# Capacity experts: first expert's rows by a selection product, last expert's rows added by products, output stored tile by tile in the same stage

## The chip, the cores and the metric

The kernel runs on one core of a Trainium2 chip. A core has a matrix engine (TensorE), a vector engine (VectorE), a scalar engine (ScalarE), a general engine (GpSimd) and a queue engine (SyncE) that issues transfers; each has its own instruction stream, and the streams meet only at semaphores. Sixteen transfer engines (DMA) move data between DRAM and the on-chip memory SBUF. TensorE writes into eight accumulator banks (PSUM) of 128 x 512 numbers each. The metric is the time of one execution on the device, in microseconds. All numbers are f32.

## The reference, cut to what matters

Two layers of a perceiver with 8 x 64 = 512 tokens of width 512. The change lies in the very last part, a mixture of 8 experts with a fixed capacity:

```
xf = layernorm(x).reshape(512, 512)
probs = softmax(xf @ Wr);  topk_probs, topk_experts = top_k(probs, 2)
cap = ceil(512 * 2 * 1.25 / 8)              # 160
y = zeros
for e in range(8):
    gate = sum(where(topk_experts == e, topk_probs, 0), -1)
    vals, idx = top_k(where(chosen by e, gate, -inf), cap)
    g = where(isfinite(vals), vals, 0)
    y = y.at[idx].add(g[:, None] * (relu(xf[idx] @ W1[e]) @ W2[e]))   # W1 512x2048, W2 2048x512
out = x + y
```

Each token goes to two experts at most; an expert takes the 160 tokens with the highest gates.

## The kernel before, in words

The program is a row of stages, each with its own tiles and semaphores. At the end of a stage all engines meet, its semaphores are cleared, and they meet again. `capacity_experts` (line 1839) is the last stage that computes; `write_out` (L3033) is a stage of its own that stores `x`, 1 MB, with one transfer and waits for it (L3041).

Tokens lie in 4 tiles (`NT`) of 128 partitions. The stage begins with the norm of `x` into `hn`; SyncE stores `hn` into the DRAM tensor `dispatched` (L1934). TensorE turns `hn`, computes the router's logits (L2149), VectorE makes the gates (`gate`), TensorE spreads each expert's gates over all partitions (L2157), and ScalarE copies them out as `gate_rows`.

For an expert e, `place_tokens(e)` on VectorE (L2010 to L2020) counts for each token how many tokens come before it, and makes `pick`: for each of the four token tiles a matrix of 128 tokens by 160 slots, 1 where the token has that slot. `list_tokens(e)` on TensorE (L2168) multiplies `pick` with gates and token numbers into the bank `meta`; `take_tokens(e)` on VectorE (L2031, L2032) copies each slot's gate and token number. With the numbers GpSimd gathers the expert's rows out of `dispatched`, 128 rows and 32 rows (L1964). `turn_rows(e)` on TensorE (L2181) turns them into the banks `turned`, and `put_picked(e)` on VectorE (L2039) copies them into `picked_T`.

The order on TensorE for each expert is written out by hand at the end of the function: `wide` 0 to 5 (L2198), 64 products of 160 columns against W1 in groups of 12, the last one of 4; between them `turn_y(e - 1)`, and after the third group `list_tokens(e + 1)`; after the sixth `turn_rows(e + 1)`; then `down` 0 and 1 (L2213), 48 and 16 such products against W2. (The calls are the same for each expert; before expert 0 stand `list_tokens(0)` and `turn_rows(0)`.) ScalarE copies each group out of its bank (L2100, L2110), and in `put_y(e)` scales the turned output rows with the slot's gate (L2120) and stores them into the DRAM tensor `expert_rows` (L2124). VectorE's order is also written by hand: `place_tokens(0)`, `take_tokens(0)`, `place_tokens(1)`, `put_picked(0)`, and then per expert the next ones' steps. `find_slots` computes for each token the rows in `expert_rows` of its two experts: the greater and the lesser number, 0 (a row of zeros) where there is none.

At the end GpSimd gathers, per token tile, first the lesser slot's rows (k = 1) and then the greater's (k = 0) (L1976), and VectorE adds them to `x` (L2076). The gathers of k = 1 wait until experts 0 to 6 are stored, those of k = 0 until all are.

SyncE loads the weights in chunks of 2 MB, three places for each of W1 and W2 (L1920, L1926); a chunk's place is free when the products that read it are done.

Of the kernel before, what the change touches and what calls it, by code (L numbers as in the profile page):

```python
# [1838 lines left out]
def capacity_experts(g):  # L1839
# [12 lines left out]

    W1_READ, W2_READ = (3, len(TRIPLES)), (len(TRIPLES) + 1, N_RING)
    with Stage(nc, "f") as s:
        w1 = s.sb("w1", [P, CHUNKS, KD, F // 2])
# [31 lines left out]
        slot = s.sb("slot", [P, TOP, NT], mybir.dt.uint32)  # L1887
        back = s.sb("back", [P, NT, D])
        ring = [s.ps(f"ring{i}", [P, 512]) for i in range(3)]
        meta = s.ps("meta", [P, 512])  # L1890
        turned = [s.ps(f"turned{i}", [P, 512]) for i in range(2)]
        y_back = [s.ps(f"y_back{i}", [P, D]) for i in range(2)]
        acc = turned + y_back
        r_in = s.sem("r_in")
        w1_in = [s.sem(f"w1_in{i}") for i in range(CHUNKS)]
# [14 lines left out]
        gathered = [s.sem(f"gathered{t}") for t in range(NT)]  # L1910
        added = s.sem("added")
        block = s.block()

        @block.sync
        def _(sp):
# [24 lines left out]
            for e in range(E_N):  # L1940
                for n in (2 * e + 3, 2 * e + 4):
                    if n < 2 * E_N:
                        load_w1(n)
                for n in (2 * e + 3, 2 * e + 4):
                    if n < 2 * E_N:
                        load_w2(n)

        @block.gpsimd
        def _(pool):
# [6 lines left out]
            pool.wait_ge(hn_stored, 16)  # L1956
            for e in range(E_N):
                pool.wait_ge(tokens_ready, e + 1)
                if e >= 2:

                    pool.wait_ge(picked_full, e - 1)
                for j, (lo, hi) in enumerate(PARTS):
                    m = hi - lo
                    pool.indirect_dma_start(out=rows_in[0:m, e % 2, j, :], out_offset=None, in_=g.dispatch_dram[:, :],  # L1964
                                            in_offset=bass.IndirectOffsetOnAxis(ap=token[0:m, e % 2, j:j + 1], axis=0)
                                            ).then_inc(rows_landed[e % 2], 16)
            pool.wait_ge(slots_ready, 1)
            pool.wait_ge(zero_stored, 16)
            for k in (1, 0):

                pool.wait_ge(y_stored[0], 32 * E_N // 2)
                pool.wait_ge(y_stored[1], 32 * (E_N // 2 - k))
                for t in range(NT):
# [7 lines left out]
        def _(dve):  # L1981
# [41 lines left out]
            def take_tokens(e):  # L2023
                dve.wait_ge(tokens_full, e + 1)
                if e >= 2:

                    dve.wait_ge(rows_landed[e % 2], 32 * (e // 2))
                    dve.wait_ge(y_out, 2 * (e - 1))
# [7 lines left out]
            def put_picked(e):  # L2036
                dve.wait_ge(picked_full, e + 1)
                for j, (lo, hi) in enumerate(PARTS):
                    dve.tensor_copy(picked_T[:, e % 2, :, lo:hi],  # L2039
# [3 lines left out]
            def find_slots():  # L2043
# [8 lines left out]
                own.wait()  # L2052
                own.did(dve.tensor_reduce(slot_f[:, 0, :], kept[:], AXX, ALU.max))
                own.did(dve.tensor_reduce(slot_f[:, 1, :], kept[:], AXX, ALU.add))
                own.wait()
# [3 lines left out]

            place_tokens(0)  # L2060
            take_tokens(0)
            place_tokens(1)
            put_picked(0)
            for e in range(E_N):
# [8 lines left out]
            for k in (1, 0):  # L2073
                for t in range(NT):
                    dve.wait_ge(gathered[t], 16 * (2 - k))
                    dve.tensor_tensor(g.x[:, t, :], back[:, t, :], g.x[:, t, :], ALU.add).then_inc(added, 1)  # L2076

        @block.scalar
        def _(act):
# [33 lines left out]
            def put_y(e):  # L2113
                act.wait_ge(tokens_ready, e + 1)
                for j, (lo, hi) in enumerate(PARTS):
                    m = hi - lo
                    act.wait_ge(y_full, 2 * e + j + 1)
                    if e >= 2:
                        act.wait_ge(y_stored[e % 2], 32 * (e // 2))
                    act.activation(y[0:m, e % 2, j, :], y_back[j][0:m, :], ACT.Copy, scale=slot_gate[0:m, e % 2, j:j + 1]  # L2120
                                   ).then_inc(y_out, 1)
                act.wait_ge(y_out, 2 * e + 2)
                for j, (lo, hi) in enumerate(PARTS):
# [3 lines left out]
            for e in range(E_N):  # L2127
# [4 lines left out]
                for n in range(2, len(TRIPLES)):  # L2132
                    put_hidden(e, n)
                for j in range(len(DOWN)):
                    put_y_T(e, j)
            put_y(E_N - 1)

        @block.tensor
        def _(pe):
# [21 lines left out]
            def list_tokens(e):  # L2161
# [8 lines left out]
                last.then_inc(tokens_full, 1)  # L2170

            def turn_rows(e):
                pe.wait_ge(rows_landed[e % 2], 32 * (e // 2 + 1))
                if e >= 1:
                    pe.wait_ge(picked_out, 2 * e)
                else:
                    pe.wait_ge(rows_out, E_N)
                for j, (lo, hi) in enumerate(PARTS):
# [39 lines left out]
            def turn_y(e):  # L2218
# [3 lines left out]
                for j, (lo, hi) in enumerate(PARTS):  # L2222
                    for k in range(KD):
                        last = pe.transpose(y_back[j][0:hi - lo, k * P:(k + 1) * P], y_T[:, k, lo:hi], g.ident[:])  # L2224
                    last.then_inc(y_full, 1)

            pe.wait_ge(numbered, 1)
            list_tokens(0)
            turn_rows(0)
            for e in range(E_N):  # L2230
# [11 lines left out]
                for j in range(len(DOWN)):  # L2242
                    down(e, j)
            turn_y(E_N - 1)

# [786 lines left out]

def write_out(g):  # L3033
    nc = g.nc
    with Stage(nc, "z") as s:
        stored = s.sem("stored")
        block = s.block()

        @block.sync
        def _(sp):  # L3040
            sp.dma_start(tokens(g.out), g.x[:]).then_inc(stored, 16)  # L3041
            sp.wait_ge(stored, 16)


def constants(g):
# [18 lines left out]
def build(nc, dram, out, stages=range(6)):  # L3064
    with ExitStack() as ctx:
# [23 lines left out]
        if 5 in stages:  # L3089
            capacity_experts(g)  # L3090
        write_out(g)

# [94 lines left out]
```

## Time and profile before

| | us |
|---|---|
| median of three runs | 2594.85 (2593.65 to 2602.11) |
| profiled execution, its time | 2598.24 |
| profiled execution, span from the first to the last instruction | 2596.5 |
| the stage of the capacity experts and the output store | about 2222 to 2596.5 |

The busy shares, the chain of waits and the timelines are of that profiled execution. Its time is 1.7 us longer than its span. An f32 product of the code stands in the trace as two instructions of TensorE, a transpose as one. "Idle before" in a timeline row is the time that the engine stood still ahead of the row, and the arrow names what ended it.

### The profile page before, as it was taken

Reading aid. Unit: us, or ns where it says so; the run is one execution under the profiler, and the core shown is the slowest. Engines: PE = TensorE matmul, PEld = TensorE weight load, DVE = VectorE, ACT = ScalarE, POOL = GpSimd, SP = SyncE. Lnnn points to the kernel's source line nnn. Section 1 sums busy time; section 2 is a strip of 40 time slices with the busy share of each in tenths; the row PEclk is TensorE's granted clock in tenths of the full one; section 3 lists DMA queues with packets and bytes.
Section 4 is the critical chain, followed back from the end, with each engine's and each line's share of the span. In section 5 each row is a group of like instructions: output and inputs, shape, how many; then the busy total and the mean of one; then the engine's idle time right before and its main releaser. Section 6 shows DMA issues by size and latency. Waiting matters only on the chain. (4 is left out here: it accounts for less than half of the span.)

```text
span 2596.5 us, 26998 instructions
## 1 busy us (share of the span) xinstructions
PE 2236.0 (86%) x10194; PEld 1341.1 (52%) x10194; DVE 1044.8 (40%) x2135; ACT 735.0 (28%) x1462; POOL 421.4 (16%) x477
## 2 busy tenths in 40 slices
PE   5799999999999885799999878776898966599996
PEld 2355555555555433444444435444454434499996
DVE  4345655655655025200000258777294035422110
ACT  2334544544444112211111143342153101111111
POOL 0000000000000000489993111222000000000001
PEclk8999999999999997799999988776899987799998
DMA  5001222122121220868877364231400010556552
GB/s 193 26 15 47 72 74 64 52 75 75 41 70 54 93 73 21 315 261 315 314 309 282 131 212 134 95 114 39 171 33 16 0 66 2 218 210 242 218 207 92
DMA packets 131539, 327.33 MB, mean 126 GB/s; under 512 B 39857, under 2 KB 89170, under 8 KB 111827
## 3 DMA queue, kind: packets, MB, share of 16 engines
q1 hardware_dynamic: 99392, 297.20, 31.7%
q10 hardware_dynamic: 29202, 19.49, 2.4%
q0 software_dynamic: 2816, 8.92, 1.0%
q8 instruction: 83, 1.36, 0.2%
q14 instruction: 46, 0.37, 0.0%
HBM read 303.22 MB, written 21.24 MB: 125 GB/s over the span
## 5 line engine op out<-in xcount | busy, mean ns | idle before, releaser
L868 PE MATMUL a_mix<-a_xn,a_probs_T 128*128 128x384 f32 (+1 forms) x832 | 313.4, 493 | 14.3 <-issue 10.2
L797 PE MATMUL a_sc<-a_wk_centred,a_ctx_T 128*128 128x512 f32 x624 | 288.3, 599 | 4.3 <-DVE a_keys L462 2.3
L1774 PE MATMUL c_gate_up<-c_w_wide,c_h_rows 128*128 128x512 f32 x480 | 210.9, 592 | 0.0
L868 PEld LDWEIGHTS a_mix<-a_xn,a_probs_T 128*128 128x128 f32 (+1 forms) x832 | 145.5, 191 | 119.8 <-issue 72.3
L797 PEld LDWEIGHTS a_sc<-a_wk_centred,a_ctx_T 128*128 128x128 f32 x624 | 117.9, 192 | 129.2 <-issue 106.0
L1679 DVE TENSOR_TENSOR c_hidden<-c_silu,c_gate_up 128x512 f32<-128x512 f32 x38 | 26.1, 688 | 355.1 <-PE c_gate_up L1774 343.3
L2198 PE MATMUL f_ring<-f_picked_T,f_w 128*128 128x160 f32 x1024 | 146.6, 304 | 1.0 <-DVE f_picked_T L2039 1.0
L1774 PEld LDWEIGHTS c_gate_up<-c_w_wide,c_h_rows 128*128 128x128 f32 x480 | 90.1, 190 | 108.1 <-issue 108.1
L462 DVE SCALAR_TENSOR_TENSOR a_keys<-a_k_bias,a_std,a_sc 128x512 f32<-128x512 f32 (+1 forms) x104 | 77.1, 742 | 167.6 <-PE a_sc L797 167.6
L2198 PEld LDWEIGHTS f_ring<-f_picked_T,f_w 128*128 128x128 f32 x1024 | 142.9, 193 | 1.3 <-DVE f_picked_T L2039 1.1
L2213 PE MATMUL f_ring<-f_hidden,f_w 128*128 128x160 f32 x1024 | 141.2, 300 | 0.4 <-ACT f_hidden L2100 0.4
L2213 PEld LDWEIGHTS f_ring<-f_hidden,f_w 128*128 128x128 f32 x1024 | 139.3, 190 | 0.9 <-ACT f_hidden L2100 0.6
L1817 PE MATMUL c_y<-c_w_down,c_hidden_T 128*128 128x512 f32 x304 | 138.9, 601 | 0.0
L616 ACT ACTIVATE a_sq<-a_keys 128x512 f32<-128x512 f32 (+1 forms) x104 | 65.6, 630 | 195.3 <-DVE a_keys L462 195.3
L421 POOL TENSOR_SCALAR a_mask<-a_mask 128x896 bf16<-128x896 uint8 x8 | 7.5, 937 | 614.6 <-DVE a_top L491 596.5
L2707 PE MATMUL d_mean<-d_share,d_scores 128*128 128x64 f32 (+1 forms) x416 | 75.3, 372 | 33.3 <-issue 24.3
L491 DVE CUSTOM_DVE_ANT_0 a_probs<-a_sc,a_mask 128x896 f32<-128x896 f32 x64 | 67.3, 1088 | 82.1 <-PE a_sc L828 82.1
L2707 PEld LDWEIGHTS d_mean<-d_share,d_scores 128*128 128x128 f32 (+1 forms) x416 | 74.0, 284 | 34.5 <-issue 24.5
L2542 POOL TENSOR_TENSOR d_scores<-d_scores,d_left 128x1601 f32<-128x1601 f32 x16 | 54.0, 3374 | 213.1 <-ACTq L2616 212.8
L2560 DVE MAX8 d_best<-d_left 128x8 f32<-128x1601 f32 x48 | 87.6, 1826 | 1.4
L2564 DVE MATCH_REPLACE8 d_left<-d_best,d_left 128x1601 f32<-128x1601 f32 x48 | 86.9, 1811 | 0.0
L1817 PEld LDWEIGHTS c_y<-c_w_down,c_hidden_T 128*128 128x128 f32 x304 | 55.9, 194 | 56.4 <-issue 56.4
(489 smaller groups left out, 3505.6 us busy)
## 6 DMA issues: line engine op xcount, KB each, us to landing
c_w_wide<-in_L_ffn_W SPq DMA_DIRECT2D x68, 1024.0 KB, 7.0
f_w<-in_L_ffn_W SPq DMA_DIRECT2D x32, 2048.0 KB, 9.5
c_w_down<-in_L_ffn_W SPq DMA_DIRECT2D x34, 1024.0 KB, 7.5
a_ctx_T<-in_ctx_T SPq DMA_DIRECT2D x48, 384.0 KB, 3.6
a_xn<-in_ctx SPq DMA_DIRECT2D x24, 768.0 KB, 6.4
d_context_T<-in_ctx_T SPq DMA_DIRECT2D x24, 768.0 KB, 10.5
d_context<-in_ctx SPq DMA_DIRECT2D x8, 2304.0 KB
mixed_context<-a_mixed_T ACTq DMA_DIRECT2D x84, 64.0 KB, 1.8
```

Of the source, the lines that this page charges most:

```text
L462: dve.scalar_tensor_tensor(out=keys[0:m, n % 4, :], in0=k_bias[0:m, :], scalar=std[0:m, t:t + 1], in1=key_bank(b, t)[0:m, :], op0=ALU.mult ...
L491: dve.tensor_tensor_reduce(out=probs[:, n % 2 * 2 + h, :].rearrange("p (c n) -> p c n", c=2), in0=sc[h][:, :, 0:BANK], in1=mask[:].rearran ...
L616: act.activation(sq[0:m, n % 2, :], keys[0:m, n % 4, :], ACT.Square).then_inc(squared, 1)
L797: last = pe.matmul(key_bank(b, t), ctx_T[:, n % AHEAD, k, cols], wk_centred[:, k, :], start=(k == 0), stop=(k == KC - 1))
L868: ins = pe.matmul(mix[:, 0:DC], probs_T[0:m, t, p * P:(p + 1) * P], xn[0:m, b % 2, t, :], start=(t == 0), stop=(t == CT - 1))
L1774: last = pe.matmul(gate_up[2 * (u % 2) + part][:], h[:, k, :], w_wide[:, i % WIDE_RING, k, :], start=(k == 0), stop=(k == KD - 1))
L1817: last = pe.matmul(y[t % 2][:], hidden_T[:, u % 2, k, :], w_down[:, i % DOWN_RING, k, :], start=(c == 0 and k == 0), stop=(c == 1 and k == ...
L2198: last = pe.matmul(ring[use % 3][:, (m - lo) * CAP:(m - lo + 1) * CAP], w1[:, i % CHUNKS, k, at:at + P], picked_T[:, e % 2, k, :], start=( ...
L2213: last = pe.matmul(ring[use % 3][:, (m - lo) * CAP:(m - lo + 1) * CAP], w2[:, i % CHUNKS, k, at:at + P], hidden[:, k, :], start=(k == 0), ...
L2560: own.did(dve.max(eight, src))
L2564: ins = dve.match_replace(left[:, r, :], eight, src, MASKED)
L2707: last = pe.matmul(mean[t // 8][0:m, t % 8, :], scores[:, b % KEEP, r, t * P:t * P + m], share[:, r, :], start=(r == 0), stop=(r == 1))
```

## The change

Three things are changed, all at the two ends of the last stage.

The first expert's rows are no longer gathered. TensorE multiplies `hn` (as weights, 128 tokens by 128 features) with `pick` of expert 0 (160 columns), 4 x 4 products, which gives the rows already turned in the banks `turned`. GpSimd's gathers begin with expert 1; the buffers and waits are counted accordingly.

The last expert's rows are no longer stored and gathered. Its `pick` is turned by eight transposes between the two `down` steps, ScalarE copies it out as `pick_T`, and at the end eight products of 512 columns (4 token tiles, slots in two parts of 128 and 32) put the scaled rows into four banks, which VectorE adds to `x`. `find_slots` leaves out the last expert, so the k = 1 gathers need the rows of experts 0 to 5, and the k = 0 gathers those of 0 to 6.

The output is stored by SyncE in four transfers, one per tile after its last addition, inside the stage; the stage `write_out` is gone.

```diff
+    LAST = E_N - 1
+    def landed(e):
+        return 32 * (e // 2 + e % 2)
+        pick_T = s.sb("pick_T", [P, 2, TOK])
+        put = [turned[0], turned[1], meta, ring[0]]
 # SyncE, behind the weight loads
+            for t in range(NT):
+                sp.wait_ge(summed, t + 1)
+                sp.dma_start(tokens(g.out)[:, t, :], g.x[:, t, :]).then_inc(stored, 16)
+            sp.wait_ge(stored, 16 * NT)
 # GpSimd
-            for e in range(E_N):
+            for e in range(1, E_N):
                 pool.wait_ge(tokens_ready, e + 1)
-                if e >= 2:
+                if e >= 3:
                     pool.wait_ge(picked_full, e - 1)
...
             for k in (1, 0):
-                pool.wait_ge(y_stored[0], 32 * E_N // 2)
-                pool.wait_ge(y_stored[1], 32 * (E_N // 2 - k))
+                pool.wait_ge(y_stored[0], 32 * (E_N // 2 - k))
+                pool.wait_ge(y_stored[1], 32 * (E_N // 2 - 1))
 # VectorE
-                    dve.wait_ge(rows_landed[e % 2], 32 * (e // 2))
+                    if e >= 3:
+                        dve.wait_ge(rows_landed[e % 2], landed(e - 2))
...
             def put_picked(e):
                 dve.wait_ge(picked_full, e + 1)
+                if e == 0:
+                    for j, (lo, hi) in enumerate(((0, 3), (3, KD))):
+                        dve.tensor_copy(picked_T[:, 0, lo:hi, :], turned[j][:, 0:(hi - lo) * CAP]
+                                        .rearrange("p (k n) -> p k n", k=hi - lo)).then_inc(picked_out, 1)
+                    return
...
-                own.did(dve.tensor_reduce(slot_f[:, 0, :], kept[:], AXX, ALU.max))
+                own.did(dve.tensor_reduce(slot_f[:, 0, :], kept[:, :, 0:LAST], AXX, ALU.max))
...
             place_tokens(0)
+            put_picked(0)
             take_tokens(0)
             place_tokens(1)
-            put_picked(0)
...
+            dve.wait_ge(added, 2 * NT)
+            for t in range(NT):
+                dve.wait_ge(put_full, t + 1)
+                dve.tensor_tensor(g.x[:, t, :], put[t][:], g.x[:, t, :], ALU.add).then_inc(summed, 1)
 # ScalarE: put_y(LAST) returns after the scaling; no store
-                for j in range(len(DOWN)):
-                    put_y_T(e, j)
+                put_y_T(e, 0)
+                if e == LAST:
+                    act.wait_ge(pick_turned, 1)
+                    for j, (lo, hi) in enumerate(PARTS):
+                        act.activation(pick_T[0:hi - lo, j, :], turned[j][0:hi - lo, :], ACT.Copy).then_inc(pick_T_out, 1)
+                put_y_T(e, 1)
 # TensorE
+            def pick_rows():
+                pe.wait_ge(rows_out, E_N)
+                pe.wait_ge(picks_ready, NT)
+                for k in range(KD):
+                    j, at = divmod(k * CAP, 3 * CAP)
+                    for t in range(NT):
+                        last = pe.matmul(turned[j][:, at:at + CAP], g.hn[:, t, k * P:(k + 1) * P], pick[:, 0, t, :],
+                                         start=(t == 0), stop=(t == NT - 1))
+                last.then_inc(picked_full, 1)
...
+            def turn_pick():
+                pe.wait_ge(picked_out, 2 * E_N)
+                for j, (lo, hi) in enumerate(PARTS):
+                    for t in range(NT):
+                        last = pe.transpose(turned[j][0:hi - lo, t * P:(t + 1) * P], pick[:, LAST % 2, t, lo:hi],
+                                            g.ident[:])
+                last.then_inc(pick_turned, 1)
+
+            def put_rows():
+                pe.wait_ge(pick_T_out, 2)
+                pe.wait_ge(tokens_ready, E_N)
+                for j, (lo, hi) in enumerate(PARTS):
+                    pe.wait_ge(y_out, 2 * LAST + j + 1)
+                    for t in range(NT):
+                        last = pe.matmul(put[t][:], pick_T[0:hi - lo, j, t * P:(t + 1) * P], y[0:hi - lo, LAST % 2, j, :],
+                                         start=(j == 0), stop=(j == 1))
+                        if j == 1:
+                            last.then_inc(put_full, 1)
+
             pe.wait_ge(numbered, 1)
+            pick_rows()
             list_tokens(0)
-            turn_rows(0)
...
                 for j in range(len(DOWN)):
                     down(e, j)
-            turn_y(E_N - 1)
+                    if e == LAST and j == 0:
+                        turn_pick()
+            turn_y(LAST)
+            put_rows()
 # build
-        write_out(g)
```

## Rows read from the trace of the kernel before

**Rows 1.** The page, busy time, share of the span and instructions of each engine.

```profile
PE 2236.0 (86%) x10194; PEld 1341.1 (52%) x10194; DVE 1044.8 (40%) x2135; ACT 735.0 (28%) x1462; POOL 421.4 (16%) x477
```

**Rows 2.** The chain of waits in order of time: start, duration in us, what.

```profile
2243.64 0.77 DVE f_compared L2010 x2
...
2250.17 0.95 DVE f_pick L2020 x4
```

**Rows 3.** Timeline of TensorE, capacity stage: start, duration in us, instructions [idle before].

```profile
2241.86 1.97 PE L2157 MATMUL f_turned<-ident,f_gate 128*128 128x128 f32 x8 [4.20 <-DVEq L2000]
...
2251.26 1.55 PE L2168 MATMUL f_meta<-f_gate,f_pick 128*128 128x2 f32 x16 [4.02 <-DVE f_pick L2020]
2263.76 1.68 PE L2181 MATMUL f_turned<-ident,f_rows_in 128*128 128x128 f32 x8 [10.95 <-DMA f_rows_in<-dispatched,f_token]
2266.42 13.07 PE L2198 MATMUL f_ring<-f_picked_T,f_w 128*128 128x160 f32 x72 [0.98 <-DVE f_picked_T L2039]
...
2288.76 1.02 PE L2181 MATMUL f_turned<-ident,f_rows_in 128*128 128x128 f32 x8 [0.33 <-DMA f_rows_in<-dispatched,f_token]
2289.71 17.65 PE L2213 MATMUL f_ring<-f_hidden,f_w 128*128 128x160 f32 x128
...
2405.86 1.02 PE L2181 MATMUL f_turned<-ident,f_rows_in 128*128 128x128 f32 x8 [2.06 <-DMA f_rows_in<-dispatched,f_token]
...
2521.42 1.02 PE L2181 MATMUL f_turned<-ident,f_rows_in 128*128 128x128 f32 x8 [1.43 <-DMA f_rows_in<-dispatched,f_token]
```

**Rows 4.** Windows: stretch, length, engines' busy time; last three: granted clock, DMA share, GB/s.

```profile
2245.00:2246.00 1.00, 1.00 (x10) 1.00 (x9) 0.94 (x4) 0.79 (x2) 0.00 (x0) 0.84 1.00 426
2251.00:2252.00 1.00, 0.74 (x7) 0.77 (x7) 0.12 (x1) 0.00 (x0) 0.00 (x0) 1.00 1.00 426
2252.00:2253.00 1.00, 0.81 (x11) 0.71 (x10) 0.15 (x3) 0.00 (x0) 0.00 (x0) 0.57 0.96 410
...
2266.40:2272.65 6.25, 6.23 (x23) 6.23 (x24) 0.00 (x0) 0.00 (x0) 0.00 (x0) 0.50 0.00 0
...
2273.00:2274.00 1.00, 1.00 (x9) 1.00 (x9) 0.00 (x0) 0.57 (x1) 0.00 (x0) 1.00 0.00 0
...
2579.00:2580.00 1.00, 0.00 (x0) 0.00 (x0) 0.00 (x0) 0.00 (x0) 0.00 (x0) 0.91 0.41 158
```

**Rows 5.** The weights' tile, its loads issued between 2224 and 2232.

```profile
DMA to landing us min/median/max: 10.3/20.6/32.6
```

**Rows 6.** Groups by line and shape (count, busy us, mean ns), and one timeline row of VectorE.

```profile
L1347 PE MATMUL e_ring<-e_wo,e_o_T 128*128 128x512 f32 x32 | 14.0, 595 | 0.7 <-ACT e_o_T L1266 0.7
...
L2039 DVE COPY f_picked_T<-f_turned 128x512 f32<-128x512 f32 x8 | 5.5, 690 | 21.0 <-PE f_turned L2181 21.0
...
L2039 DVE COPY f_picked_T<-f_turned 128x128 f32<-128x128 f32 x8 | 2.2, 280 | 0.0
...
2221.04 0.69 DVE L1235 TENSOR_TENSOR x<-e_ring,x 128x512 f32<-128x512 f32 x1 [2.74 <-PE e_ring L1347]
```

**Rows 7.** The chain of waits at the end, in order of time.

```profile
2576.72 0.67 PE f_y_back L2224 x4
...
2578.05 0.67 ACT f_y L2120
...
2579.10 1.90 DMA expert_rows<-f_y
...
2585.79 3.71 DMA f_back<-expert_rows,f_slot
...
2589.53 0.69 DVE x L2076
```

**Rows 8.** SyncE's timeline, and transfers by line: size in KB, median us from issue to landing.

```profile
2591.46 0.40 SPq L3041 DMA_DIRECT2D out<-x  x1
...
expert_rows<-f_y ACTq DMA_DIRECT2D x8, 256.0 KB, 2.1
...
out<-x SPq DMA_DIRECT2D x1, 1024.0 KB, 4.3
```

More of the change, by code:

```diff
@@ L1910, in capacity_experts @@
         gathered = [s.sem(f"gathered{t}") for t in range(NT)]
-        added = s.sem("added")
+        added, pick_turned, pick_T_out = s.sem("added"), s.sem("pick_turned"), s.sem("pick_T_out")
+        put_full, summed, stored = s.sem("put_full"), s.sem("summed"), s.sem("stored")
         block = s.block()
@@ L2052, in find_slots @@
                 own.wait()
-                own.did(dve.tensor_reduce(slot_f[:, 0, :], kept[:], AXX, ALU.max))
-                own.did(dve.tensor_reduce(slot_f[:, 1, :], kept[:], AXX, ALU.add))
+                own.did(dve.tensor_reduce(slot_f[:, 0, :], kept[:, :, 0:LAST], AXX, ALU.max))
+                own.did(dve.tensor_reduce(slot_f[:, 1, :], kept[:, :, 0:LAST], AXX, ALU.add))
                 own.wait()
@@ L2121, in put_y @@
                                    ).then_inc(y_out, 1)
+                if e == LAST:
+                    return
                 act.wait_ge(y_out, 2 * e + 2)
@@ L2133, in _ @@
                     put_hidden(e, n)
-                for j in range(len(DOWN)):
-                    put_y_T(e, j)
-            put_y(E_N - 1)
+                put_y_T(e, 0)
+                if e == LAST:
+                    act.wait_ge(pick_turned, 1)
+                    for j, (lo, hi) in enumerate(PARTS):
+                        act.activation(pick_T[0:hi - lo, j, :], turned[j][0:hi - lo, :], ACT.Copy).then_inc(pick_T_out, 1)
+                put_y_T(e, 1)
+            put_y(LAST)
         @block.tensor
@@ L2170, in list_tokens @@
                 last.then_inc(tokens_full, 1)
-            def turn_rows(e):
[L2173 to L2177, printed above, removed]
+            def pick_rows():
[7 more added lines that the diff above has]
+                last.then_inc(picked_full, 1)
+            def turn_rows(e):
+                pe.wait_ge(rows_landed[e % 2], landed(e))
+                pe.wait_ge(picked_out, 2 * e)
                 for j, (lo, hi) in enumerate(PARTS):
@@ L3030, in _ @@
             ss.on_gpsimd(pool)
[L3033 to L3042, printed above, removed]
 def constants(g):
```

## The prediction

> **What bounds the kernel now.** I read the busy shares first: TensorE is busy for 86% of the span, VectorE for 40%, ScalarE for 28% [rows 1]. The reader is to see that no other engine can be the bound on average, and that this says nothing yet of the two ends of the last stage, which is where the change works.
>
> Then the chain of waits, in order of time, and TensorE's timeline beside it. Before the first expert the chain goes through VectorE (eight comparisons, then four picks, ready at 2251.13), a small product on TensorE that lists the tokens, and GpSimd's two gathers [rows 2, 3]. The list is done at 2252.8, the turning of the gathered rows starts at 2263.76 after 10.95 us of idle time, and the first weight product at 2266.42. From there to about 2577.8 TensorE runs almost without a break: seven more gathers leave four gaps, 0.33 us the first, 2.06 the longest, 1.43 the last, 4.2 us in all [rows 3]. The end of the chain is again not TensorE: turning the last expert's output back (2576.72), scaling on ScalarE (to 2578.72), store to DRAM (1.90), four gathers, the last one landing 3.71 us after its issue, and the last addition, 2589.53 to 2590.22 [rows 7]. The output store is issued at 2591.46 and takes 4.3 us, and the span ends at 2596.5, 0.74 us later [rows 8].
>
> The granted clock is the third view. After TensorE began to turn the gates at 2241.86 it rose at about 2245.2; it is 1.00 when the list starts and falls to half (1.2 GHz) within the next microsecond, after TensorE had idled for 4.0 us. After the long wait it is 0.50 until 2272.65: the first 23 instructions took 6.23 us, 0.27 us each. At 2.4 GHz 128 of them take 17.65 us, 0.138 each [rows 3, 4]. One thing has to be seen in the counts: 36 products of the first three groups stand there as 72 instructions [rows 3]. An f32 product is two passes; a transpose is one.
>
> **The head: the first expert's rows by a product.** Removed from the path: two gathers, eight turnings. Added: 16 products of 160 columns, so 32 instructions, from 2251.26 on, where the list started before. Bounds: 32 at 0.138 are 4.4 us, 32 at 0.27 are 8.7. Until the clock falls, at about 2252.15, six run at 0.138; at half clock some 13 more run until 2255.6, where I let it rise, since TensorE works without a break here and the turning of the gates got the clock back in 3.4 us [rows 3, 4]; the last 13 take 1.8 us: done at 2257.3. The list follows (1.3 to 1.56 us): 2258.7. VectorE's two copies out of the banks (480 and 160 elements, about 0.95 us by the copies of 512 and 128 at 0.69 and 0.28 [rows 6]) run beside the list and end at 2258.3, hidden by 0.4 us; were the cover gone, they would cost 0.95. First weight product at 2258.7 instead of 2266.42: **7.7 us gained**.
>
> The clock gives the rest. The first 72 instructions took 13.07 us, where 72 at 0.138 are 9.9 [rows 3]. If the clock is up before they start, **3.2 us** more are gained; if it stays low as long behind their start as before, nothing, and then the selection is the slow one too. So the head gives 10.9; its bounds are 5.8 (the 8.7 us selection and a low clock behind it) and 12.6 (no fall at all: 1.7 us less than I count for the selection).
>
> What is late next? The weights: the six chunks issued from 2224 to 2232 land 10.3 to 32.6 us after their issue, the last by about 2264 [rows 5]. The first expert's second chunk is wanted 64 instructions after the start, at 2267: cost 0. The picks of the second expert: VectorE now waits for the selection before it takes the tokens, and behind that waiting copy are queued the first token list and the placing of expert 1, 7.5 us (2243.64 to 2251.13 for the same work [rows 2]). Tokens taken at 2259.1, placed at 2266.6; TensorE wants them after 72 instructions, at 2268.6: hidden by 2.0 us, and by more at a lower clock. Seven gathers stay, each beside 56 instructions as before, 7.7 us; I take their 4.2 us of gaps as unchanged.
>
> **The gathers into the output.** The lesser slot's four gathers need no row of expert 6 any more and go out right behind those of the last expert's rows, in the same GpSimd queue, one expert earlier. Nothing on TensorE's path waits for them, and all eight additions from gathers end before the last product. Cost 0; if they delay the rows in front, the price of rival 2. The reductions over seven experts in place of eight: 0.
>
> **The tail: the last expert's rows by products.** Between the two halves of the last down-projection TensorE gets eight transposes, 1.02 us in the row of eight [rows 3]; I take 0.9, on the path. ScalarE's two copies of them (0.67 us each, as its scaling [rows 7]) lie beside the 32 instructions that follow, 4.4 us: 0. The turning back starts at 2577.6, and the first scaled part is out at 2579.05 (the second scaling started at 2578.05 before [rows 7], plus 0.9 and a little). Then come eight products of 512 columns, 16 instructions at 14.0/32 = 0.44 us [rows 6]: 7.0 us, with 0.15 for the drain of the last (0.595 long, 0.44 apart), to 2586.2. The second part's scaling ends beside the first four. VectorE adds a tile out of its bank in 0.69 us [rows 6], less than the 0.875 in which TensorE fills the next, so only the last addition follows: 2586.9, where it was 2590.22. The gain is small because 7.15 + 0.7 us of products and addition replace 1.90 + 3.71 us of transfers, the gathers' issues and an addition.
>
> The output goes in four stores of 256 KB; only the last is on the path. Such a store landed in 2.1 us, one of 1 MB in 4.3 [rows 8]. The stage's exit, which stood between the last addition and the store (1.24 us with the entry of the next stage), now comes behind the store, where the exit was 0.74 us; I take 1.0. End: 2586.9 + 2.1 + 1.0 = 2590.0: **6.4 us gained** (6.7 with an exit of 0.74). The products' clock is the open term: in the trace it is still up after the turning and has begun to fall before 2580 [rows 4], when TensorE had stood still for 2 us. It now works there, so I take it as held. If it falls for 3.4 us and comes back as in the head, 1.7 us are lost; if it falls and stays low, 6.1, and the tail gives 0.3.
>
> **Sum.** 7.7 + 3.2 + 6.4 = 17.3 us. The profiled execution took 2598.24 us (span 2596.5 and 1.7 around it): 2580.9. It lies 3.4 us above the median of the three runs with the same work on the path, so the predicted time is 2594.85 - 17.3 = **2577.5 us**. Own range of this case, with the difference between runs of one kernel: 2573 to 2581.
>
> **The rivals.**
> 1. The clock is low at both ends: 5.8 in the head and 0.3 in the tail: 6.1, 2588.8 us, no change that can be measured. For it: the trace fell at just these two places [rows 4]. Against: TensorE then had nothing to do. The Trainium skill speaks for it: "TensorE: Matmul & The Clock Gate", section "A second HAM failure mode: psum-queue depth-cycling", tells of a kernel whose short idle times between groups of products make the clock swing. By that rule the tail's products, which stand behind short waits for ScalarE, would run at half clock at least in part; no row here shows it; both falls in these rows stand behind idle times of 2 us and more.
> 2. The lesser slot's gathers collide with the last expert's rows: 4 x 128 rows more while a weight chunk is also under way. Price: what the first gather paid when the transfer engines were full [rows 4], 10.95 us of idle TensorE in place of 1.43 [rows 3], 9.5 us. Against: they are queued behind. 2587.0 us.
> 3. Only the tail's clock falls and stays low: 10.9 + 0.3 = 11.2: 2583.7 us.
> 4. Slower than before: the seven gathers left come late and the clock falls at each. With the first gather's 10.95 us against the cover of 7.7 each leaves 3.2 us, and a fall behind it costs 3.2 more, as at the first expert: 6.4 for each of seven, 45 less the 4.2 there are, against 17.3 gained: 2618 us. It decides from the fourth of the seven on (4 x 6.4 = 25.6 against 21.5). Against: they have the same products and the same weight loads beside them as before, and their longest gap is 2.06 us.
> 5. More than forecast: no fall in the head and the short exit, 12.6 + 6.7 = 19.3: 2575.6 us.
>
> **How the numbers follow.** Chances: forecast 0.58, rival 1 0.09, rival 2 0.08, rival 3 0.10, rival 4 0.03, rival 5 0.12. No change means within 0.3% (7.8 us), about what a measurement of this kernel can tell: rival 1 with a part of rival 2, which lies on the border, 0.12. Slower: rival 4, 0.03. Faster: 0.85. The range reaches from below rival 5, by a few microseconds in which runs of one kernel differ (2593.65 to 2602.11 before), to rival 2's border: 2571 to 2586.
>
> **What would show it.** Right: no gather before the first weight product, which starts 7.4 us after the first selection instruction and runs at 0.138 from the start; no idle time before the second expert's list; 16 instructions of 512 columns at the end, 0.44 apart; the last store landing 2 us after its issue; 12.8 us from the last weight product to the end of the span instead of 20.2. Wrong: granted clock 0.5 in the first group or in the last products, idle time before the second expert's list (VectorE late), a gap of several microseconds before the last expert's rows are turned, or an exit far over 1 us.

## The result: 13 us faster by the medians, 15.7 us in the stage of the two profiles

| | median, us | range | ratio to before, 95% interval |
|---|---|---|---|
| before, 8 runs | 2594.25 | 2590.33 to 2606.17 | |
| changed, 8 runs | 2580.85 | 2575.23 to 2591.23 | 0.9948 [0.9925, 0.9971] |
| before, beside e1 to e4, 23 runs | 2601.43 | 2592.01 to 2605.20 | |
| changed again (e4 below), 6 runs | 2584.78 | 2578.86 to 2588.73 | 0.9943 [0.9921, 0.9964] |

The ratio is that of the times beside each other on one chip, and not exactly the quotient of the medians. The predicted gain of 17.3 us lies inside the interval (7.5 to 19.5 us). The predicted time was 2577.5; the median is 3.4 us above it. The runs of one kernel differ by 16 us, and most of that seems to arise before the stage that was changed: in the thirteen profiles of this study it starts anywhere from 2218.4 to 2233.5 us, though the code ahead of it is the same, while the stage took 358.2 and 355.4 us in the two profiles of the changed kernel. So times are compared here from the stage's first instruction (the norm's statistics on VectorE) to the end of the span. The page of the changed kernel, busy shares as in [rows 1]:

```profile
span 2579.9 us, 27075 instructions
PE 2248.7 (87%) x10242; PEld 1349.2 (52%) x10242; DVE 1047.1 (41%) x2139; ACT 736.6 (29%) x1464; POOL 419.8 (16%) x475
```

TensorE is busy 12.7 us longer than before (1.7 of that in a slow row, see below) and the kernel is faster: most of its added work stands where the core waited. Its timeline answers to [rows 3] (start, duration, instructions, idle time ahead):

```profile
2250.35 6.26 PE L2207 MATMUL f_turned<-f_pick,hn 128*128 128x160 f32 x32 [3.82 <-DVE f_pick L2033]
2256.44 1.29 PE L2197 MATMUL f_meta<-f_gate,f_pick 128*128 128x2 f32 x16
2257.66 10.05 PE L2234 MATMUL f_ring<-f_picked_T,f_w 128*128 128x160 f32 x72
2267.55 1.29 PE L2197 MATMUL f_meta<-f_gate,f_pick 128*128 128x2 f32 x16
...
2277.01 1.02 PE L2217 MATMUL f_turned<-ident,f_rows_in 128*128 128x128 f32 x8 [0.36 <-DMA f_rows_in<-dispatched,f_token]
...
2509.26 1.02 PE L2217 MATMUL f_turned<-ident,f_rows_in 128*128 128x128 f32 x8 [1.50 <-DMA f_rows_in<-dispatched,f_token]
2510.20 19.33 PE L2249 MATMUL f_ring<-f_hidden,f_w 128*128 128x160 f32 x128
...
2561.33 1.04 PE L2267 MATMUL f_turned<-ident,f_pick 128*128 128x128 f32 x8
2562.20 4.51 PE L2249 MATMUL f_ring<-f_hidden,f_w 128*128 128x160 f32 x32
2567.11 1.09 PE L2260 MATMUL f_y_back<-ident,f_y_T 128*128 128x128 f32 x8 [0.39 <-ACT f_y_T L2133]
2568.69 1.96 PE L2277 MATMUL f_turned<-f_y,f_pick_T 128*128 128x512 f32 x4 [0.48 <-ACT f_y L2143]
...
2572.29 1.98 PE L2277 MATMUL f_turned<-f_y,f_pick_T 32*128 32x512 f32 x4
...
2574.97 1.02 PE L2277 MATMUL f_ring<-f_y,f_pick_T 32*128 32x512 f32 x2
```

Three things are to be seen. The first weight product comes 7.31 us after the first selection instruction, with no idle time between, where 15.16 us lay before; 72 instructions then take 10.05 us, not 13.07. The second expert's list follows with no idle time ahead of it, so VectorE was in time. And one row is worse than any of before: the 128 down instructions of expert 6 take 19.33 us instead of 17.65; such a group is called slow in what follows.

The end, VectorE's last additions and the output's stores (transfers: size in KB, median us to landing), beside [rows 7, 8]:

```profile
2573.52 1.48 DVE L2099 TENSOR_TENSOR x<-f_turned,x 128x512 f32<-128x512 f32 x2 [24.01 <-PE f_turned L2277]
2575.16 0.69 DVE L2099 TENSOR_TENSOR x<-f_meta,x 128x512 f32<-128x512 f32 x1 [0.17 <-PE f_meta L2277]
2576.02 0.69 DVE L2099 TENSOR_TENSOR x<-f_ring,x 128x512 f32<-128x512 f32 x1 [0.17 <-PE f_ring L2277]
...
out<-x SPq DMA_DIRECT2D x4, 256.0 KB, 2.0
```

Additions wait for TensorE (0.17 us each); the last ends at 2576.71, 10.0 us after the last weight instruction (2566.71) instead of 13.9, and the span ends 3.2 us later instead of 6.3. The two profiles add up:

| part of the span | before | changed | difference |
|---|---|---|---|
| ahead of the stage | 2222.62 | 2221.70 | -0.9 |
| stage's start to first selection or list instruction | 28.64 | 28.65 | 0 |
| to the first weight product | 15.16 | 7.31 | -7.9 |
| first 72 weight instructions | 13.07 | 10.05 | -3.0 |
| from there to the last weight instruction | 296.8 | 299.0 | +2.2 |
| to the last addition | 13.9 | 10.0 | -3.9 |
| to the end of the span | 6.3 | 3.2 | -3.1 |

Of the +2.2 us, 0.9 are the eight transposes and 1.7 the slow row, less 0.4 of shorter gaps.

The -3.0 us of the first 72 instructions hold for this profile of the kernel before. e2 and e3 (below) keep its head as it was, and there the same 72 took less, because the clock came back 3.5 and 2.9 us after their start and not 6.25 us after it [rows 4]. TensorE's timeline of e2, a window of it (the third number from the end is the granted clock), and the timeline of e3:

```profile
2262.08 11.69 PE L2212 MATMUL f_ring<-f_picked_T,f_w 128*128 128x160 f32 x72 [0.98 <-DVE f_picked_T L2043]
```

```profile
2265.00:2266.00 1.00, 1.00 (x7) 1.00 (x6) 0.00 (x0) 0.00 (x0) 0.00 (x0) 0.77 0.00 0
```

```profile
2267.57 11.44 PE L2202 MATMUL f_ring<-f_picked_T,f_w 128*128 128x160 f32 x72 [0.98 <-DVE f_picked_T L2043]
```

From the first list instruction to the end of the 72, the old head took 28.2, 26.7 and 26.4 us in the three profiles that have it, and the new one 17.4 (18.4 in e1): 9.1 to 10.9 us for the head of the changed kernel, by the execution that one compares with.

### The profile page after: what moved, and what is told of

Its sections match the earlier page's. It is cut to its first block and busy times, and to the rows that moved or that the text cites. A ratio compares the mean times of both kernels' runs of the same rounds, so it can differ in the third digit from the quotient of the medians.

```text
span 2579.9 us, 27075 instructions
## 1 busy us (share of the span) xinstructions
PE 2248.7 (87%) x10242; PEld 1349.2 (52%) x10242; DVE 1047.1 (41%) x2139; ACT 736.6 (29%) x1464; POOL 419.8 (16%) x475
## 5 line engine op out<-in xcount | busy, mean ns | idle before, releaser
L868 PE MATMUL a_mix<-a_xn,a_probs_T 128*128 128x384 f32 (+1 forms) x832 | 315.1, 496 | 13.9 <-issue 9.8
```

Of the source, the lines that this page charges most:

```text
L868: ins = pe.matmul(mix[:, 0:DC], probs_T[0:m, t, p * P:(p + 1) * P], xn[0:m, b % 2, t, :], start=(t == 0), stop=(t == CT - 1))
```

## The experiments

Each run is told by its ratio to the kernel before on the same chip and by the stage of its profiled execution. The columns: stage's start to the end of the span; first selection or list instruction to the first weight product; first 72 weight instructions; the gaps ahead of the turned rows of experts 1 to 7, summed; down groups of 128 that took 19.33 us instead of 17.65; last weight instruction to last addition; from there to the end. There is one profile for each kernel. Pauses ahead of the down products are not among the gaps: 1.09 us in e4 and 0.61 in e9 ahead of those of expert 6, 1.49 in e5 ahead of those of the last expert, where the changed kernel has 0.39.

| kernel | ratio [95%] | stage | to weights | 72 | gaps | slow | to add | to end |
|---|---|---|---|---|---|---|---|---|
| before | | 373.9 | 15.16 | 13.07 | 4.21 | 0 | 13.9 | 6.28 |
| changed | 0.9948 [0.9925, 0.9971] | 358.2 | 7.31 | 10.05 | 3.84 | 1 | 10.0 | 3.19 |
| e1 head only | 0.9943 [0.9924, 0.9962] | 361.6 | 8.37 | 10.05 | 2.22 | 0 | 13.6 | 6.28 |
| e2 tail product | 0.9986 [0.9970, 1.0001] | 370.8 | 15.01 | 11.69 | 4.22 | 1 | 10.0 | 6.06 |
| e3 store tiles | 0.9994 [0.9977, 1.0011] | 369.3 | 14.98 | 11.44 | 2.88 | 0 | 15.8 | 3.13 |
| e4 changed again | 0.9943 [0.9921, 0.9964] | 355.4 | 7.32 | 10.05 | 1.42 | 0 | 10.4 | 3.18 |
| e5 gathers late | 0.9948 [0.9929, 0.9966] | 355.1 | 7.32 | 10.05 | 1.21 | 0 | 10.2 | 3.21 |
| e6 kept warm | 0.9947 [0.9925, 0.9968] | 358.3 | 5.65 | 10.05 | 5.16 | 1 | 10.0 | 3.19 |
| e7 list early | 0.9941 [0.9918, 0.9964] | 351.8 | 7.32 | 10.05 | 0 | 0 | 10.2 | 3.18 |
| e8 all three | 0.9932 [0.9910, 0.9955] | 349.7 | 5.65 | 10.05 | 0.28 | 0 | 10.0 | 3.24 |
| e9 one store | 0.9957 [0.9941, 0.9973] | 357.2 | 7.32 | 10.05 | 1.39 | 0 | 10.3 | 5.41 |
| e10 warm twice | 0.9930 [0.9914, 0.9946] | 350.2 | 5.65 | 10.05 | 0.72 | 0 | 10.0 | 3.25 |
| e11 all three again | 0.9924 [0.9908, 0.9939] | 350.1 | 5.64 | 10.05 | 0.67 | 0 | 10.0 | 3.25 |

### e1: the head alone

The kernel before with `pick_rows`, gathers from expert 1 on, and VectorE's new order:

```diff
-            list_tokens(0)
-            turn_rows(0)
+            pick_rows()
+            list_tokens(0)
```

> Kernel before with the selection product alone; last expert and output as before. Theory (the parts add up): the first weight product 7.3 us after the first selection instruction and the first 72 weight instructions in 10 us, so the profile 10.9 us shorter between the picks and the second expert's list, ratio to before about 0.9958. Rival (the tail's change carries the gain, the head's is given back as longer gaps before the turning of the later experts' rows): the gaps of experts 1 to 7 add up to 10 us and more instead of 4, ratio 1.000.

The stage is 12.3 us shorter, 9.8 of it at the place of the change (15.16 + 13.07 against 8.37 + 10.05), and the gain was not given back as gaps: 2.2 us. The rival is refuted. The theory holds but for 1.1 of its 10.9 us: the first weight product comes 8.37 us after the selection's start and not 7.3. The ratio can't tell e1 from the whole change. The selection took 1.06 us longer than in the changed kernel. The windows say why (the third number from the end is the granted clock):

```profile
2256.00:2257.00 1.00, 0.00 (x0) 0.00 (x0) 0.93 (x7) 0.00 (x0) 0.00 (x0) 0.56 1.00 426
2257.00:2258.00 1.00, 0.61 (x2) 0.64 (x3) 0.25 (x2) 0.00 (x0) 0.00 (x0) 0.50 1.15 492
...
2262.00:2263.00 1.00, 1.00 (x5) 1.00 (x5) 0.00 (x0) 0.00 (x0) 0.00 (x0) 0.52 1.07 459
2263.00:2264.00 1.00, 1.00 (x10) 1.00 (x9) 0.00 (x0) 0.00 (x0) 0.00 (x0) 1.00 1.15 492
```

Here the clock had fallen before the selection began and came back at 2263.0, 5.6 us after; in the changed kernel it fell during it:

```profile
2250.00:2251.00 1.00, 0.65 (x5) 0.68 (x6) 0.20 (x1) 0.00 (x0) 0.00 (x0) 1.00 0.88 377
2251.00:2252.00 1.00, 1.00 (x8) 1.00 (x8) 0.00 (x0) 0.00 (x0) 0.00 (x0) 0.82 1.11 475
2252.00:2253.00 1.00, 1.00 (x6) 1.00 (x5) 0.00 (x0) 0.00 (x0) 0.00 (x0) 0.50 1.04 442
...
2255.00:2256.00 1.00, 1.00 (x9) 1.00 (x8) 0.00 (x0) 0.00 (x0) 0.00 (x0) 0.97 1.04 442
```

### e2: the last expert's product alone

The kernel before with `turn_pick`, `put_rows` and the reductions over seven experts; the output stored by `write_out`.

> Kernel before with the last expert's rows put back by products alone; gathers for all other experts, output stored in its own stage. Theory: last weight product to last addition 9.9 to 10 us instead of 13.9, 0.9 us given back for the eight transposes, so 3 us net, ratio 0.9988. Rival (eight f32 products are as dear as the round trip through DRAM): distance 13 us or more, ratio 1.000 or above. In both the lesser slot's gathers move ahead; if these alone cause the clock to fall once after the last expert's rows, this run shows a slower stretch of 3.4 us in the down products of expert 6.

13.9 us became 10.0, less 0.87 for the transposes: 3.0 us, as the theory said, in the profile; the interval of the ratio (0.9970 to 1.0001) doesn't exclude that nothing was gained. Products cost less than the way through DRAM, though eight f32 products of 512 columns take 7.3 us. One slow group is there, but not behind the last expert's rows: it stands in expert 3, behind a gap of 1.89 us, long before any gather into the output.

### e3: the store by tile alone

```diff
+            for t in range(NT):
+                sp.wait_ge(added, NT + t + 1)
+                sp.dma_start(tokens(g.out)[:, t, :], g.x[:, t, :]).then_inc(stored, 16)
+            sp.wait_ge(stored, 16 * NT)
```

> Kernel before with only the output stored by tile in the capacity stage, last expert by gathers. Theory: the last addition to the end of the span takes 2.1 us for the last store and 1.0 for the exit, 3.1 us instead of 6.3, so 3.2 us, ratio 0.9988. Rival (the four stores cost as much as one, since each pays its fixed time): 5 to 6 us, ratio 0.9998.

The last addition to the end is 3.1 us, exactly as forecast, and yet the theory fails for the whole: the last addition itself comes 1.9 us later after the last weight instruction (15.8 us). The additions, whose last wait was 0.53 us before the change, now wait longer and longer for the gathers (0.81, 1.05 and 2.12 us):

```profile
2583.33 0.69 DVE L2080 TENSOR_TENSOR x<-f_back,x 128x512 f32<-128x512 f32 x1 [24.70 <-DMA f_back<-expert_rows,f_slot]
2583.77 1.07 POOL L1980 DMA_INDIRECT f_back<-expert_rows,f_slot  x1 [0.30 <-issue]
2584.05 6.39 SPq L1949 DMA_DIRECT2D out<-x  x4
...
2586.57 0.69 DVE L2080 TENSOR_TENSOR x<-f_back,x 128x512 f32<-128x512 f32 x1 [1.05 <-DMA f_back<-expert_rows,f_slot]
2589.38 0.69 DVE L2080 TENSOR_TENSOR x<-f_back,x 128x512 f32<-128x512 f32 x1 [2.12 <-DMA f_back<-expert_rows,f_slot]
```

The last gather lands 5.6 us after its issue, 3.71 in [rows 7]: the first tile's store, issued at 2584.05, runs beside it. From issue to addition the four gathers took 3.3, 3.6, 4.1 and 5.6 us, against 3.4, 3.6, 3.8 and 3.7 before: the first two as before, the third 0.3 us longer and the last, which had the stores beside it nearly all the time, 1.9. In e1, where the store comes last as well, the last gather took 3.72 us. So the stores are the likely cause, though in one profile. Of 3.15 us saved at the end only 1.3 is left (scaling's end to the end of the span, 17.8 and 16.5 us), and the ratio, 0.9994, can't tell it from nothing. Only together with the product, which takes the gathers away from the end, does the store by tile pay in full: 3.0 and 1.3 us alone, 6.1 together. The parts don't add up as I had said.

### e4: the changed kernel again

> The changed kernel unchanged, beside its parts on the same chip. Theory (parts add up): the gain is the sum of the three runs before it, 10.9 + 3.0 + 3.2 = 17 us, ratio 0.9934, less 1.7 us where the clock falls once more in the middle. Rival (something in the middle eats a part in each execution): the gap ahead of the last expert's rows is longer than before and the 128 down products behind it take 19 us instead of 17.65 again, ratio 0.995.

The stage is 18.5 us shorter than before, more than the forecast's 17.3: gaps of 1.4 us, no slow group. The rival (the middle eats a part each time) is refuted; the slow group does not come in every execution. The last addition is 0.4 us later here, because the clock fell before the last products had ended (timeline, then a window):

```profile
2576.57 1.42 PE L2277 MATMUL f_ring<-f_y,f_pick_T 32*128 32x512 f32 x2
```

```profile
2577.00:2578.00 1.00, 0.99 (x2) 0.00 (x0) 0.46 (x1) 0.00 (x0) 0.00 (x0) 0.53 0.92 344
```

### e5: the lesser slot's gathers held

```diff
-                pool.wait_ge(y_stored[0], 32 * (E_N // 2 - k))
+                pool.wait_ge(y_stored[0], 32 * E_N // 2)
```

> The changed kernel with the lesser slot's gathers held until expert 6 is stored, as before the change. Theory (the gathers' time is a matter of luck with the transfer engines, not of what is queued behind them): the wait ahead of the last expert's rows stays in 0 to 2 us as in the changed kernel, whose two profiles had 1.50 and 0.21; no slower and no faster, ratio to the changed kernel 1.000. Rival (the moved gathers collide with the last expert's rows): this wait falls to under 0.3 us, the down products of expert 6 take 17.65, the time falls by 1 to 3 us.

Stage 355.1 us against 355.4 and 358.2. The wait ahead of the last expert's rows is 0.19 us. With the gathers moved ahead it was 1.50, 0.21, 1.25 (e2), 1.13 (e6) and 0 (e9); with them late 1.43, 0, 0.54 and 0.19. That excludes a collision of 9.5 us, as rival 2 had it, and not one of half a microsecond. Between its own theory and rival the run does not decide: a wait under 0.3 us, 17.65 us for the down products behind it and a stage 0.3 to 3.1 us shorter fit both. The slow group stood behind the last expert's rows in two of five profiles with the gathers moved ahead (changed, e6) and in none of four with them late, which is too few to tell.

### e6: TensorE kept busy while it waits for the picks

```diff
+            for i in range(10):
+                pe.matmul(ring[0][:, 0:CAP], g.ident[:], g.hn[:, i % NT, 0:CAP], start=True, stop=True)
             pick_rows()
```

> The changed kernel with ten idle products of 160 columns into an unused bank while TensorE waits for the first picks (their result is not used). Theory (the selection's 6.3 to 7.3 us is 4.4 of work and a fall of the clock, caused by the 4 us of idle time ahead of it): the granted clock stays 1.00 from the turning of the gates into the weight products, the selection takes 4.4 us, the first weight product comes 5.5 us after the first selection instruction instead of 7.3 to 8.4; 1.9 us or more off the time. Rival (the f32 selection is slow by itself, the weights being another tile each time): it still takes 6 us and more at a granted clock of 1.00.

The timeline of TensorE, then the windows:

```profile
2258.10 2.88 PE L2284 MATMUL f_ring<-hn,ident 128*128 128x160 f32 x20
2262.09 4.58 PE L2207 MATMUL f_turned<-f_pick,hn 128*128 128x160 f32 x32 [1.11 <-DVE f_pick L2033]
2266.52 1.29 PE L2197 MATMUL f_meta<-f_gate,f_pick 128*128 128x2 f32 x16
```

```profile
2258.00:2262.00 4.00, 2.99 (x23) 2.74 (x21) 3.77 (x13) 1.06 (x3) 0.00 (x0) 1.00 1.00 426
2262.00:2267.00 5.00, 4.91 (x38) 4.94 (x38) 0.28 (x1) 0.00 (x0) 0.00 (x0) 1.00 1.00 429
```

The clock stays at 2.4 GHz through the selection, which takes 4.6 us where it took 6.26 and 7.31: the first weight product comes 5.65 us after the selection's start, 1.7 us sooner. Of the 6.26 us, 1.7 were the clock and nothing of the products; e8, e10 and e11 show the same 4.58 us. The rival (slow by itself) is refuted. In this execution the middle gave it back (5.2 us of gaps, one slow group), so the stage's length does not show it; e8 and e11 do.

### e7: the token list one group earlier

```diff
                 wide(e, 1)
+                if 1 <= e < LAST:
+                    list_tokens(e + 1)
                 wide(e, 2)
-                if e + 1 < E_N:
+                if e == 0:
                     list_tokens(e + 1)
```

> The changed kernel with the token list of experts 2 to 7 made one group of weight products earlier (3.3 us). Theory (what the middle loses is gathers that come after 56 instructions of cover, and a fall of the clock behind the longer ones): the waits ahead of the turned rows are zero for experts 2 to 7, every 128 down instructions take 17.65 us, 2 to 5 us faster than the changed kernel. Rival (the gathers only land later, because they meet the load of the next chunks): the same waits, no change.

All seven waits are gone, every group takes 17.65 us, and the stage is 351.8 us, 3.6 to 6.4 less than the changed kernel's. The rival falls: the gathers land in time once they are asked for 3.3 us sooner. In the medians the gain over the changed kernel is not to be seen (ratio 0.9941 against 0.9948 and 0.9943).

### e8 and e11: all three

The edits of e6 and e7, and `turn_pick` ahead of the last expert's down products, where TensorE waits 0.4 us for ScalarE.

> The changed kernel with the idle products, the early list, and the last expert's pick turned ahead of its down products, in the pause in which TensorE waits for ScalarE (0.4 us). Theory: 1.9 (clock held) + 3 (waits gone) + 0.4 (pause used) = 5 us faster than the changed kernel, ratio to the kernel before 0.992. Rival (they share one cause and don't add up): no better than the better of the two runs before it.

> The kernel with the three edits once more, more rounds. Theory: stage's start to its end 350 us instead of 355 to 358 in the changed kernel and 374 before; ratio to the kernel before 0.991, the whole of it in this stage. Rival: the rest of the program varies more than these 8 us, and the ratio lies above 0.994.

Stage 349.7 and 350.1 us; ratios 0.9932 and 0.9924, median 2577.08 us in e11's six runs beside 2598.33 of the kernel before. The kernel beats the one before by 24 us in the stage and the changed one by 5 to 8.5 us, and it beats e7 by 1.7 to 2.1: so the rival of e8 falls, the edits do add up. The ratio of e11 lies between what its theory and its rival said. The intervals of the ratios overlap those of the changed kernel (0.9943, 0.9948), so that gain over the change rests on the stage's length, which e7, e8, e10 and e11 show alike. The one gap left (0.28 and 0.67 us) is that of expert 1, whose list could not move.

### e9: one store of 1 MB in the same stage

```diff
-            for t in range(NT):
-                sp.wait_ge(summed, t + 1)
-                sp.dma_start(tokens(g.out)[:, t, :], g.x[:, t, :]).then_inc(stored, 16)
-            sp.wait_ge(stored, 16 * NT)
+            sp.wait_ge(summed, NT)
+            sp.dma_start(tokens(g.out), g.x[:]).then_inc(stored, 16)
+            sp.wait_ge(stored, 16)
```

> The changed kernel with the output stored by one transfer of 1 MB after the last addition, still inside the capacity stage. Theory (the tail's saving on the store is the size of the last transfer, not the stage that is gone): the store takes 4.3 us and the exit 1.1, so 5.3 us from the last addition to the end instead of 3.2 in the changed kernel and 6.1 to 6.3 with a stage of its own. Rival (the stage that is gone saves it): 3.5 us.

5.41 us from the last addition to the end: the theory holds (5.3), the rival (3.5) is refuted. So of the 2.9 us between e2 (6.06) and the changed kernel (3.19), 2.2 are the smaller last transfer and 0.65 the stage that is gone.

### e10: idle products ahead of the gates too

Six more idle products while TensorE waits for the first gates.

> The kernel with the three edits (idle products, early list, pick turned in the pause) and six further idle products while TensorE waits for the first gates (their result is not used). Theory: the clock rises before the gates are turned, the first four of these take 0.9 us less 0.3, and the picks come 0.3 to 0.5 us earlier after the stage's start than the 28.64 us of all runs so far, the rest as in the kernel with the three edits; 0.4 us faster, not to be told by the time. Rival: the products are still running at half clock when the gates are ready and delay them, 28.7 us and more.

The picks come 28.64 us after the stage's start, as in eleven of the other twelve profiles to 0.02 us: nothing gained, and the theory falls. (In e1, without such products, they came after 28.30 us: there the clock stood high for more of the router's products, which took 4.30 us and not 4.71 as in the changed kernel.) TensorE's timeline shows why nothing was gained, the turning of the gates still ran at half clock:

```profile
2246.30 3.55 PE L2182 MATMUL f_ring<-hn,ident 128*128 128x160 f32 x12
2250.65 1.97 PE L2188 MATMUL f_turned<-ident,f_gate 128*128 128x128 f32 x8 [0.80 <-DVEq L2013]
```

The first turning takes 1.97 us as without the idle products [rows 3]; the fill cost nothing and brought nothing. The rival falls too: the twelve added instructions end 0.80 us before the gates are ready.

## Why the prediction came out

The direction and the mechanism hold, and the size of the two ends against the profile on which it was worked out. By its steps:

- Head, forecast 7.7 + 3.2 = 10.9 us; 7.9 + 3.0 in the profiles. The selection was to be 32 instructions, six at the high clock, then a fall and a return after some 3.4 us: the clock fell at about 2251.6, after some nine instructions, and returned at 2255.1, and the selection took 6.1 us to the list against 6.0 forecast. That the fall lay as forecast is in part luck: in e1 it came before the selection, and the selection took 7.31 us, all but the last eleven instructions at half clock. The bound of 4.4 is nearly e6's 4.58. The 3.2 us for the clock behind the start belong to the one execution on record: against e2 and e3 they would be 1.6 and 1.4.
- VectorE late for the second expert: no idle time ahead of the list in any run.
- Tail, forecast 6.4: 3.9 and 3.1 less 0.9 for the transposes are 6.1. The products took 7.3 us, the last store 2.0 us, the exit 1.2. From the last weight product to the end of the span it was 13.2 us against 12.8 forecast. The open term went the forecast's way: the clock held through the products and fell at about 2575.9, as the last one ended. In four of the ten profiles with these products (e4, e5, e7, e9) it fell up to 0.9 us before their end, at a cost of 0.2 to 0.4 us. In the windows of the changed kernel:

```profile
2574.00:2575.00 1.00, 1.00 (x4) 0.40 (x3) 0.90 (x2) 0.00 (x0) 0.00 (x0) 1.00 0.00 0
2575.00:2576.00 1.00, 0.98 (x3) 0.15 (x1) 0.69 (x1) 0.00 (x0) 0.00 (x0) 0.96 0.83 307
2576.00:2577.00 1.00, 0.00 (x0) 0.00 (x0) 0.69 (x1) 0.00 (x0) 0.00 (x0) 0.50 0.87 322
```

- So rival 1 is refuted for the tail, and with it what was drawn from the Trainium skill ("TensorE: Matmul & The Clock Gate", section "A second HAM failure mode: psum-queue depth-cycling"): pauses of 0.39 and 0.48 us between the groups did not keep the clock low here; at most the last products lost it. Rival 1's head is refuted as well: the first 72 instructions took 10.05 us in every profile with the selection.
- Two prices of that rival don't follow from its rows. With 8.7 us for the selection the head would give 5.0 us and not 5.8, and sixteen instructions at twice 0.44 us would cost the tail 7.0 us and not 6.1. Both make rival 1 slower still and change nothing in the forecast.
- The middle, forecast as unchanged, is where the first profile lost: 1.7 us by a fall of the clock behind the longest gap. The step "I take their 4.2 us of gaps as unchanged" was too dear and blind to that fall: with the head changed and the lists at their old place, the gaps were 3.84, 2.22, 1.42, 1.21, 5.16 and 1.39 us, 2.5 on average, where the three profiles with the old head have 4.21, 4.22 and 2.88. Rival 4 named a late gather and then a fall, and that did happen, once in seven experts and not four times. That the gap is the cause of the fall is not shown: three of the nine profiles with gaps in the middle have a slow group, and none of the four in which the lists were moved.
- Rival 2: of its 9.5 us there is no trace (1.50 us at most ahead of the last expert's rows).

The two ends gave 17.0 us where 17.3 were forecast, and the medians still differ by only 13.4. Some 1.5 to 1.8 us of that are the head of the one profile on which the forecast was worked out: against e2's and e3's heads the two ends give 15.5 and 15.2. The rest lies within the spread of the middle and of the stages ahead, about which no experiment was made; that the medians came as close as they did is also a matter of that spread.

## What to carry to other kernels

A selection matrix that is already there can replace a gather at the first and the last step of a pipeline, where nothing covers the gather; in the middle it hides behind other work. Count f32 products as two instructions each, and look for the clock ahead of them, not only for their length. Splitting the final store paid in full here only where no gather was still under way: two changes at one end must be tried together as well as apart.

## What was not expected of the hardware

- Whether the clock falls behind a short gap is not settled by the length of the gap. Behind the waits ahead of the turned rows it fell after 1.13 (e6), 1.50 (changed) and 1.89 us (e2), each time for about 3.4 us and at a cost of 1.7, and held after 1.25 (e2), 1.43 and 2.06 (before) and 1.68 (e3), and after the 1.49 us of e5 ahead of the down products. In the changed kernel it came 1.8 us after the gap had ended, while TensorE was working:

```profile
2510.00:2511.00 1.00, 1.00 (x10) 0.96 (x10) 0.69 (x2) 0.00 (x0) 0.00 (x0) 1.00 0.12 45
2511.00:2512.00 1.00, 1.00 (x7) 1.00 (x6) 1.00 (x4) 0.00 (x0) 0.00 (x0) 0.53 0.02 8
...
2514.00:2515.00 1.00, 1.00 (x8) 1.00 (x7) 0.00 (x0) 0.00 (x0) 0.00 (x0) 0.76 0.04 8
```

- Products with 32 rows as weights cost the same as with 128: 1.98 us for four instructions of 512 columns in the second part, 1.96 in the first.
- Idle products cost nothing where TensorE waits anyway: ten of them, 2.88 us in a pause of 3.9, and the picks came at the same 28.64 us. With the ten the clock, which was high already, stayed high (e6); the six ahead of the gates, begun at half clock, did not raise it in time (e10).
